# Sequence convolution and adapter product: where VectorE makes the late magnitudes' product and the next angles

## The reference

```python
kernel = 2 * Re( sum_n C_n (exp(dtA_n) - 1) / A_n * exp(dtA_n * l) )     # [64, 1024], 64 states n
y = causal_conv(x * mask, kernel) + (x * mask) * D                        # mask: l < length[b]
x = x + y * mask
x = x + einsum('bsi,boi->bso', x, weight[adapter_ids])
```

## Time and profile before

| | |
|---|---|
| median of 3 runs | 362.64 us (360.56 to 363.25) |
| the profiled execution | 363.85 us, span of its instructions 362.1 us |
| PE busy | 312.5 us, 86% of the span |
| DVE, ACT, POOL busy | 209.7, 152.0, 108.6 us |
| moved by DMA | 81.54 MB, mean 225 GB/s |
| one mask instruction (L817), mean of 64 | 0.474 us |
| strips, issue to landing, median | 8.6 us |
| mean granted clock of TensorE | 0.967 |

### The profile page before, as it was taken

How to read it: one execution, slowest core, us unless ns; L and a number is a source line. 1 busy time by engine, 2 the same in 40 slices (tenths; PEclk the granted TensorE clock), 3 DMA queues, 4 the chain that set the end, 5 groups by cost and what they waited for, 6 DMA issues and landing times.

```text
span 362.1 us, 8259 instructions
## 1 busy us (share of the span) xinstructions
PE 312.5 (86%) x2584; PEld 273.9 (76%) x2585; DVE 209.7 (58%) x353; ACT 152.0 (42%) x210; POOL 108.6 (30%) x133
## 2 busy tenths in 40 slices
PE   0055749997998986898999999999999999999993
PEld 0054649997988986797888888888888888888882
DVE  5979466887678747296733942692122692096200
ACT  1947383535264331404435821853312852273200
POOL 4024215386363842376003400420000520160000
PEclk9998598998999999899999999999999999999998
DMA  7894779979999999992049216802107813942222
GB/s 264 319 366 143 237 259 415 412 261 371 416 396 378 357 394 411 393 336 87 2 109 392 81 29 238 343 15 72 48 10 253 326 22 94 366 155 58 61 59 58
DMA packets 20550, 81.54 MB, mean 225 GB/s; under 512 B 4464, under 2 KB 4656, under 8 KB 16944
## 3 DMA queue, kind: packets, MB, share of 16 engines
q1 hardware_dynamic: 18272, 80.98, 60.6%
q10 hardware_dynamic: 2256, 0.30, 0.5%
HBM read 72.58 MB, written 18.64 MB: 252 GB/s over the span
## 4 chain that ended last, share of the span: by engine, by line
PE 51%; POOL 2%; DVE 1%; issue 1%; ACT 0%; DVEq 0%; ACTq 0%
PE bank L1144 51%; POOL z L475 2%; DVE z_lo L993 0%; DVE mid L817 0%; DVE z L1043 0%; DVE o_tile L1025 0%; ACT z_hi L642 0%; DVEq L993 0%; DVEq L1024 0%; ACTq L642 0%; DVEq L815 0%; ACTq L635 0%; ACTq L687 0%
## 5 line engine op out<-in xcount | busy, mean ns | idle before, releaser
L1083 PE MATMUL bank<-x,strips 128*128 (+6 forms) x1536 | 108.6, 233 | 14.4 <-DMA strips<-k_padded 14.4
L1083 PEld LDWEIGHTS bank<-x,strips 128*128 128x128 f16 x1536 | 103.2, 101 | 19.2 <-issue 10.8
L1144 PE MATMUL bank<-w_hi,z_hi 128*128 128x512 f32 x272 | 83.8, 389 | 1.6 <-DVE z_lo L993 1.6
L1144 PE MATMUL bank<-w_lo,z_hi 128*128 128x512 f32 x272 | 83.8, 389 | 0.0
L1144 PE MATMUL bank<-w_hi,z_lo 128*128 128x512 f32 x272 | 83.7, 389 | 0.0
L475 POOL TENSOR_TENSOR z<-z,mid 128x512 f32 (+1 forms) x31 | 52.3, 1696 | 56.7 <-DVE mid L817 56.5
L494 POOL TENSOR_TENSOR w_raw<-w_raw,ident 128x128 f32<-128x128 f32 x36 | 32.2, 915 | 123.5 <-DMA w_raw<-in_w 113.9
L1144 PEld LDWEIGHTS bank<-w_hi,z_hi 128*128 128x128 f32 x272 | 51.0, 188 | 12.5 <-issue 2.0
L1144 PEld LDWEIGHTS bank<-w_lo,z_hi 128*128 128x128 f32 x272 | 51.1, 188 | 10.7
L1144 PEld LDWEIGHTS bank<-w_hi,z_lo 128*128 128x128 f32 x272 | 51.1, 188 | 10.6
L993 DVE TENSOR_TENSOR z_lo<-z,z_hi 128x512 fp32r<-128x512 f32 (+2 forms) x36 | 36.5, 1054 | 37.1 <-ACT z_hi L642 37.1
(11 more groups left out here) (165 smaller groups left out, 183.4 us busy)
## 6 DMA issues: line engine op xcount, KB each, us to landing
strips<-k_padded SPq DMA_DIRECT2D x64, 512.0 KB, 8.6
w_raw<-in_w SPq DMA_DIRECT2D x18, 1024.0 KB, 8.1
k_padded<-k_row SPq DMA_DIRECT2D x8, 1152.0 KB, 6.6
out<-o_tile SPq DMA_DIRECT2D x34, 256.0 KB
z<-in_x SPq DMA_DIRECT2D x8, 1024.0 KB, 6.3
w_raw_early<-in_w SPq DMA_DIRECT2D x2, 1024.0 KB, 10.6
k_row<-k_tile ACTq DMA_DIRECT2D x8, 32.0 KB, 6.9
small<-in_params SPq DMA_DIRECT2D x1, 192.0 KB, 2.4
```

What stands on the lines that cost most here:

```text
L1083: last = mm(conv_ps[k][:, e * COL + d * B:(e + 1) * COL], strips16[:, k, e, k_part, d, :], x16[:, bass.ds(g % 2, 1), x_part, col:col + (NB ...
L1144: last = mm(slot_ps[par][half][:, :], left_[:, par, c, :], right[:, c, half * HALF:(half + 1) * HALF], start=(c == 0 and left_ is z_hi and ...
```

## The change

Six edits. SCALED goes from 3 to 4: ScalarE makes group 3's magnitudes by itself as well, right behind those of group 2, and the product over the rest has 2048 elements a partition for 2560. The product goes from ahead of k_scaled_out(1) to behind x_scales(2), ahead of turn(1), and `rest_of_magnitudes` on ScalarE from between exchange(2) and k_high(2) to behind sum_x(3), ahead of the loop from group 4. In `turn`, angles(g+3) come first after the mask of g-1, then the parts of k, and x_low(g+1) behind k_low(g+2). At the end of the stage mask (7,2) goes ahead of the low parts of the first slot. TensorE sums x's bound of group 2 ahead of convolve(0,3) and not behind it.

```diff
--- before.py
+++ after.py
@@ -64,7 +64,7 @@
     WARM_START, WARM_MIDDLE = 26, 12
     PEEL = 4
     HALF = L // 2
-    SCALED = 3
+    SCALED = 4
 
     INV_2PI = 1.0 / (2.0 * math.pi)
     TWO_PI_HI = 6.28125
@@ -593,6 +593,7 @@
             sum_x(0)
             exchange(0)
             scaled_magnitudes(2)
+            scaled_magnitudes(3)
             k_high(0)
             store_k(0)
             x_high(0)
@@ -603,7 +604,6 @@
             store_k(1)
             sines(2)
             exchange(2)
-            rest_of_magnitudes()
             k_high(2)
             store_k(2)
 
@@ -615,6 +615,7 @@
             k_high(3)
             store_k(3)
             sum_x(3)
+            rest_of_magnitudes()
             with act.Fori(4, NG) as g:
                 sines(g)
                 exchange(g)
@@ -885,11 +886,6 @@
             link(v.tensor_tensor(mask[:, :, :], lens.unsqueeze(1).to_broadcast([P, NB, B]),
                                  t_iota.unsqueeze(2).to_broadcast([P, NB, B]), ALU.is_gt))
 
-            late = slice(SCALED * GH, H)
-            v.tensor_tensor(mag[:, :, late, :],
-                            dre[:, late].unsqueeze(1).unsqueeze(3).to_broadcast([P, 2, H - SCALED * GH, S]),
-                            power.rearrange("p (e s) -> p e s", e=2).unsqueeze(2).to_broadcast([P, 2, H - SCALED * GH, S]),
-                            ALU.mult).then_inc(e_ready, 1)
             k_scaled_out(1)
             k_low(1)
             angles(2)
@@ -901,12 +897,12 @@
 
 
                 mask_pair(g - 1, NPAIR - 1)
-                x_low(g + 1)
+                if not (isinstance(g, int) and g == NG - 3):
+                    angles(g + 3)
                 k_scaled_out(g + 2)
                 mask_pair(g, 0)
                 k_low(g + 2)
-                if not (isinstance(g, int) and g == NG - 3):
-                    angles(g + 3)
+                x_low(g + 1)
                 mask_pair(g, 1)
                 if not (isinstance(g, int) and g == NG - 3):
                     factors(g + 3)
@@ -922,6 +918,11 @@
             factors(3)
             mask_pair(0, 2)
             x_scales(2)
+            late = slice(SCALED * GH, H)
+            v.tensor_tensor(mag[:, :, late, :],
+                            dre[:, late].unsqueeze(1).unsqueeze(3).to_broadcast([P, 2, H - SCALED * GH, S]),
+                            power.rearrange("p (e s) -> p e s", e=2).unsqueeze(2).to_broadcast([P, 2, H - SCALED * GH, S]),
+                            ALU.mult).then_inc(e_ready, 1)
             turn(1)
 
 
@@ -1034,8 +1035,8 @@
             mask_pair(NG - 1, 1)
             first_slot = [field(dve, 0, f, B - 1) for f in (F_B0, F_B1)]
             dve.wait_ge(early_hi_ready, 2)
+            mask_pair(NG - 1, 2)
             low_parts(first_slot, 0, slice(0, H - GH), early_lo_ready)
-            mask_pair(NG - 1, 2)
             mask_pair(NG - 1, NPAIR - 1)
             dve.wait_ge(masked, 2 * NG * NPAIR)
             dve.wait_ge(x_loaded, NG)
@@ -1109,8 +1110,8 @@
             k_rows_made(2)
             convolve(0, 1)
             convolve(0, 2)
+            sum_x_bound(2)
             convolve(0, 3)
-            sum_x_bound(2)
             with pe.Fori(1, NG - 2) as g:
                 convolve(g, 0)
                 k_rows_made(g + 2)
```

## The result

| | before | changed |
|---|---|---|
| median | 361.65 us (360.56 to 363.25, 4 runs) | 367.37 us (365.11 to 369.83, 4 runs) |
| ratio | | 1.016, 95% interval 1.011 to 1.020 |
| the profiled execution | 363.85 us, span 362.1 | 365.62 us, span 363.9 |

The account below looks back on a forecast made before the run. Strips of k, late behind full DMA engines, bound the first stage; filling DMA holes gains. The advance ran 2.1, 1.3, 0.4, 1.4 us, the end adding 0: 362.64 - 1.4, rounded to 361.2 us, range 357.6 to 364.0.

Parts of the forecast that it names:

- Parts 1 and 2: Early groups: moving the product brings copy_rows(1) 2.1 us forward; through turn 1, 1.3 us remain at store_k(3) and copy_rows(3).
- Part 3: rest_of_magnitudes behind sum_x(3): factors(4) 2.8 us late, store_k(4) at about 85.3, 0.4 us of the 1.3 kept.
- the cover: Full DMA engines after copy_rows(3), reaching to about 93 us, hide 1.5 us of copy_rows(4)'s lateness, less 1.3.
- part 4: Turns 2 to 5: each store 0.6 to 1.5 us earlier, worth 1 us at the hole at 121; advance 1.4 us.
- rival A: Lead kept whole, TensorE waiting only for strips: 3.5 to 5.5 us gained, 357.1 to 359.1 us; chance 0.25.
- The table load itself: ScalarE's table switches for rest_of_magnitudes: 1.28 us each, the measured duration used instead of the page's about 2.7.
- Part 5: End of the first stage: mask (7,2) ahead of the low parts changes VectorE's order, not its sum; 0 us.
- rival C: At the end, GpSimd's addition of pair (7,2) holds a low part; 0.8 us lost, 362.0 us; chance 0.10.
- B: Slower: the stop at factors(4) makes copy_rows(4) later than the cover; 363 to 366 us; chance 0.15.

Follow-up runs that it names:

- e7: The changed kernel with the old order at the end, low parts ahead of mask (7,2): 1.018 of before, median 367.19 us.
- e9: Kernel before with SCALED = 4, bound's new place, product behind k_low(2), rest_of_magnitudes between sum_x(2) and sines(3), old order in turn: 0.9935 of before.
- e1b: The changed kernel with ScalarE's iteration for group 4 written out ahead of its loop: 1.014 of before, median 365.13 us.
- e0b: The changed kernel once more, unchanged, timed together with e1b: 1.020 of before, median 367.29 us.
- e2: The kernel before with the new order in turn alone: 1.005 of before (1.000 to 1.009), medians equal.
- e8b: Like e9 but with the new order in turn: 0.994 of before, median 360.3 us.
- e11: The changed kernel with rest_of_magnitudes moved to between x_high(2) and k_high(3): 1.006 of before, median 363.32 us.
- e10: Like e11, with ScalarE's iteration for group 4 also written out ahead of its loop: 1.004 of before, median 362.65 us; repeated, 1.003.
- e0: The changed kernel once more, unchanged, beside new runs of the kernel before: 1.0195 of before, median 368.15 us.
- e14: Like e10, with the product moved from behind x_scales(2) to behind k_low(2): 1.0065 of before, median 362.14 us.

## Why the prediction was wrong

**Parts 1 and 2 held as times.** Where 35.5, 37.0 and 43.5 were forecast, k_scaled_out(1) came at 35.3, store_k(1) at 36.8 and copy_rows(1) at 43.85. The scales of group 2 began at 57.7, the product took 2.28 us for 2.53, and k_scaled_out(3) came at 66.0 for 66.3. copy_rows(3) came at 74.35, within 0.5 us. That the lead of copy_rows(1) is a gain of all that follows is not borne out: in the traces of e7, e9 and e1b copy_rows(1) comes at 39.5 to 40.7, over 3 us ahead of the changed kernel's, and copy_rows(2) at 56.3 to 56.8, 2 us behind its 54.32.

**Part 3 had the mechanism and the wrong sum.** By the copies it is the greatest miss: the lead over the kernel before was to go from 1.3 us at copy_rows(3) to 0.4, and it went from 1.7 to 2.7 behind. factors(4) was forecast at 76.2 and came at 75.9. Two terms behind it were too small. From factors(4) to k_scaled_out(4) I had 6.8 to 7.7 us: the 7.7 of the old turn (81.05 - 73.36), less 3.3 for x_low and its wait, plus 2.4 to 3.3 for angles. It was 9.4. Moved against GpSimd's left(4), the small instructions of the least adapter took 0.70 and 1.18 us where 0.2 would do. angles(5) took 3.3, the upper value. store_k(4) came at 87.3 for 85.3. The second term is the cover: I gave 1.5 us less 1.3 and let copy_rows(4) come at 92.1 to 94.0. It came at 94.1, and the DMA engines ran dry from 93. My own figures, 0.6 to 2.5 us late against 0.2 of cover, leave between 0.9 ahead and 1.0 behind of the 1.3, so 0.4 was too high even without the wrong term.

**The step that failed altogether is part 4.** It let the lateness end with turn 2 and won back 1 us at 121. It isn't won back: the copies of groups 5, 6 and 7 are 3.8, 4.1 and 3.4 us behind. Late factors also make sum_x(4) late, and TensorE, which had waited almost only for strips (rival A says only; before, there are also 0.7 us for left and 0.5 for magnitudes), stood 2.2 us for left(4) and 2.46 us for the magnitudes, fell to the lower clock and took 2.7 us more for two pairs. x_high, x_scales and the masks follow those pairs, and the stores after them. store_k stays 3 to 4.5 us behind up to group 7. And I counted the table switches of rest_of_magnitudes as two. There are five: the loop is entered with the other table, and every turn loads it. That follows from the change's text, since `sines` is the first thing in the loop. I had looked only at the straight-line order. It is worth some 2 us (e0b against e1b).

**The table load itself** took 1.28 us in all rows. The figure of about 2.7 us that the Trainium skill gives ("ScalarE: Activation LUTs", What ACT_TABLE_LOAD costs) is made up of about 1.28 us for the load and 1.38 for a drain. The trace agrees with the first part and does not show the second: the exponentials end at 73.82, the load starts at 73.84, and the sine at 75.14. The figure would have pointed to the right side for the wrong reason.

**Part 5** was right in that nothing shows (the stretch from the table's matmuls to the second stage took 20.56 us for 20.23), and rival C wrong, though its mechanism is there: GpSimd's addition did get between the low parts, as the lock of the "SBUF — State Buffer" page (Who interferes with whom) in the Trainium skill has it, and e7 shows that nothing is lost by it.

**The new order in turn** was forecast to gain 1 us through earlier stores. e2 shows no gain and perhaps a loss; e8b against e9 shows none. The step that failed is that each store comes 0.6 to 1.5 us earlier. In e8b store_k(4) comes 2.65 us later than in e9, by the instructions that GpSimd's work stretches. The next three stores make up 1.2, 0.8 and 0.6 us of it, as forecast for a turn, and store_k(7) is level, 124.29 and 124.28.

The right case was B, to which I gave 0.15 and 363 to 366 us; the median of 367.4 is above even that. Its cause is settled as to place: rest_of_magnitudes directly ahead of sines(4), with the loads that it brings into the loop, is 1.4 to 1.5% of the 1.6 to 2.0% (e11 and e10 against e0). What stays open is why e10, with 1.003 to 1.004 (1.000 to 1.002 by the medians), does not reach the 0.994 of e8b. The product's place is ruled out by e14. The load for Sin ahead of sines(4), 1.28 us, the place of the exponentials and the order at the end together remain; they were not tried apart. It is not a later store: store_k(4) is at 83.07 in e14 and at 83.08 in e8b. The traces point to the late sine, which no run tests by itself. VectorE stands 2.1 us for it ahead of factors(4) in e10, e11 and e14, 0.64 in e8b, and TensorE then stands 2.3 to 2.5 us in all for VectorE's masks, in e8b not at all. In e14:

```profile
82.73 4.67 PE L1091 MATMUL bank<-x,strips 128*128 x48 [2.50 <-DVE mid L825]
```

## What to carry to other kernels

Price a piece of work that moves by what is queued behind it in its new place, on every engine that then waits, and follow it until some row shows the queue caught up; a cover (here full DMA engines) that just holds in the sum is not one. Before a piece that needs another state of the engine, such as a function table, is put ahead of a loop, look at the state in which the loop is entered and comes round: if they differ, the switch is paid in each turn. And put such a piece where both its engines stand idle in the trace: the same product and exponentials gain 0.5% in one place and lose 1.5 to 2% in another.

## What the runs showed of the hardware

One ACT_TABLE_LOAD took 1.28 us each time, with the next instruction 1.29 to 1.30 us after its start. A load that the loop's back edge does not need is still in the loop: at 90.42, 106.13 and 121.02 us. TensorE's granted clock fell to 1.2 GHz (1.00 from 88 to 89 us, 0.50 from 90 to 96) during a wait of 2.46 us, and stayed full in e10, where there was none of that kind at this place. From store_k to the copy it took 7.1 us for group 1 (36.8 to 43.85) and 6.8 for group 4 (87.3 to 94.1): as long as that even where the DMA engines went dry before its end (their share is 0.00 from 43 to 45 us). For group 1 it took 2.7 us in e7 and 3.5 in e9 and e1b, where the four strips of group 0 were issued from 36.2 us or later and not, as in the changed kernel, from 34.1, well ahead of the store. GpSimd's work stretched VectorE's small instructions of 0.2 us to 0.7 and 1.2 (e8b against e9).
